# A score convolution split by row parity, with q and k taken through device memory, in an attention layer of 4 images of 32 x 32

## The reference, cut to what matters

```python
qkv = conv1x1(batchnorm(x), qkv_w, qkv_b)            # B=4, 96 channels, 32x32
q, k, v = qkv split in 3, each 6 heads of 16 channels
qk = concat([q * 16**-0.5, k], axis=1)               # 24 images (batch x head) of 32 channels
attn = conv2d(qk, dm_w, 7x7, pad 3) + dm_b + rel_bias  # 49 scores for each pixel
attn = softmax(attn, over the 49)
out = sum over the 49 window places of attn * v shifted there
x1 = x + conv1x1(out, proj_w, proj_b)
return x1 + conv1x1(gelu(conv1x1(x1, c1_w)), c2_w)
```

## Time and profile before

| | us |
|---|---|
| median of 3 runs (1281.7 to 1283.02) | 1283.01 |
| the profiled execution, its own time | 1284.04 |
| its span from first to last instruction | 1281.9 |
| the attention layer in it, from 795.9 | 486.0 |
| DVE, POOL, PE busy in the whole span | 987.5, 920.4, 1083.4 |

### The profile page before, as it was taken

One profiled execution on the slowest core, in us unless ns is written; L12 is line 12 of the kernel. 1 busy time (PEld: TensorE's weight loads), 2 busy tenths in 40 slices (PEclk: granted clock), 3 DMA queues, 4 the chain that ended last, 5 costly groups with the idle time before them and its releaser, 6 DMA issues. The chain is left out here.

```text
span 1281.9 us, 9541 instructions
## 1 busy us (share of the span) xinstructions
PE 1083.4 (85%) x3294; PEld 369.8 (29%) x3294; DVE 987.5 (77%) x695; ACT 521.1 (41%) x548; POOL 920.4 (72%) x360
## 2 busy tenths in 40 slices
PE   7789999788989889889878695899999699990567
PEld 2233333232223233223322232233333133330122
DVE  1599999789998999989899997100969694967683
ACT  5755665786646546555646341111120111010212
POOL 0189899898979798979898955100778794979770
PEclk9889999899999999999899998699999789995678
DMA  2234354434354435543435541746495549526002
GB/s 75 84 134 150 129 166 117 150 112 152 126 151 114 160 106 148 164 140 124 159 117 138 164 138 32 155 88 111 97 161 121 112 73 191 88 55 118 20 1 70
DMA packets 107640, 150.95 MB, mean 118 GB/s; under 512 B 75451, under 2 KB 76193, under 8 KB 106825
## 3 DMA queue, kind: packets, MB, share of 16 engines
q1 hardware_dynamic: 105992, 145.01, 43.4%
q10 hardware_dynamic: 1600, 5.34, 1.4%
HBM read 123.27 MB, written 10.70 MB: 105 GB/s over the span
## 5 line engine op out<-in xcount | busy, mean ns | idle before, releaser
L691 POOL TENSOR_TENSOR hc<-h,c_rep 128x1024 f32<-128x1024 f32 x192 | 450.9, 2360 | 146.6 <-DVE h L735 136.7
L735 DVE TENSOR_TENSOR_SCAN h<-a,bu 128x1024 f32<-128x1024 f32 x192 | 439.0, 2286 | 34.2 <-POOL hc L691 15.3
L389 PE MATMUL y_ps<-hc,ident 128*128 128x512 f32 x768 | 383.1, 623 | 10.8 <-POOL hc L691 9.3
L557 ACT ACTIVATE a<-dt,a_neg 128x1024 f32<-128x1024 f32 x192 | 219.2, 1146 | 251.7 <-DVE h L735 237.6
L725 DVE TENSOR_TENSOR bu<-bu,u 128x1024 f32<-128x1024 f32 x192 | 232.1, 1209 | 17.5 <-PE bu L368 17.5
L1146 POOL TENSOR_TENSOR prod_p<-vw,at 128x3584 f32<-128x3584 f32 x18 | 130.8, 7266 | 156.5 <-DMA vw<-v_d 131.1
L389 PEld LDWEIGHTS y_ps<-hc,ident 128*128 128x128 f32 x768 | 142.7, 195 | 222.2 <-issue 178.1
L1029 PE MATMUL sc_ps<-x,w_up 128*64 128x512 f32 x672 | 179.7, 609 | 2.6 <-DMA x<-qk 2.6
L1029 PE MATMUL sc_ps<-x,w_low 96*64 96x512 f32 x672 | 178.7, 606 | 0.0
L368 PE MATMUL bu<-st,pick 96*64 96x512 bf16 (+1 forms) x512 | 118.6, 391 | 51.1 <-DVE h L735 47.4
L1167 DVE TENSOR_TENSOR acc_ps<-acc_ps,prod_v 128x512 f32<-128x512 f32 x156 | 109.1, 699 | 5.4
(11 more groups left out here) (121 smaller groups left out, 940.4 us busy)
## 6 DMA issues: line engine op xcount, KB each, us to landing
c_rep<-c_d SPq DMA_DIRECT2D x128, 512.0 KB, 3.7
c_rep<-c_d SPq DMA_DIRECT2D x128, 256.0 KB, 3.9
vw<-v_d SPq DMA_DIRECT2D x24, 532.0 KB, 9.5
x<-qk SPq DMA_DIRECT2D x72, 171.0 KB, 3.7
scores_d<-sc ACTq DMA_DIRECT2D x24, 196.0 KB
at<-scores_d SPq DMA_DIRECT2D x24, 196.0 KB, 5.3
x<-qk SPq DMA_DIRECT2D x24, 152.0 KB, 3.8
v_d<-v SPq DMA_DIRECT2D x24, 76.0 KB, 5.0
```

The lines of the kernel that those rows point to most:

```text
L389: mm = pe.matmul(y_ps[:, cols(th)], ident[:, :], hc[:, k % HC_RING, cols(th)], start=(n == 0 and d == 0), stop=(n == N_ST - 1))
L557: nc.scalar.activation(a[:, k % A_RING, :], dt[:, tile % 2, :], ACT.Exp, scale=a_neg[:, kind_of(tile), n:n + 1]).then_inc(exp_done, 1)
L691: nc.gpsimd.tensor_tensor(hc[:, k % HC_RING, :], h[:, k % H_RING, :], c_rep[:, k % C_RING, :], ALU.mult).then_inc(hc_done, 1)
L735: nc.vector.tensor_tensor_scan(scan_order(h[:, k % H_RING, :], d), scan_order(a[:, k % A_RING, :], d), scan_order(bu[:, k % 2, :], d), 0.0 ...
```

## The change

**Scores by parity.** Padded rows are kept by parity in `qk` (plane 0 odd rows, plane 1 even rows). DVE adds two planes of differences of them (2 instructions for each `differences`). With the kernel's even rows as `w_even`, its odd rows as `w_odd` and their sum `w_both`, the output rows of one parity are a product shared by both, plus one of their own: three products of 14 matmuls for a pair (42 in place of 56). ACT evicts the shared one into a third plane of `sc`, and PE adds it to each of the others with a matmul by the identity (`eye`, 128 x 128), two for a pair. The scores, and all that follows down to `o_t`, are then in the order even rows, odd rows, so each `at` and `o_d` transfer of an image becomes two of 16 partitions, and `vw` reads its rows in that order.

**q and k through memory.** The planes are stored to `qk_d` and read back: one transfer fills all 128 partitions of a plane of `x4` for one image, three for an image (128, 128 and 96 partitions of 2,432 bytes). The ring has 4 images. ACT issues these loads, but for four at the start that SP issues.

**Order.** Projections of batches 1 to 3 follow pairs 0 to 2. `exps(j)` stands behind pairs 1, 3, 6, 8 and 10, the last ahead of `mlp(2)`. `maximum(j+1)` stands ahead of DVE's last row of tile j. `differences` of batch 3 stand behind `maximum(0)`. The MLP outputs on DVE are spread over tile 4 and the end of tile 5.

**VectorE sums in two banks.** The accumulator is two PSUM banks, so three additions of 1,024 elements and one of 512 take the place of seven of 512; in the first row of a tile the product of two places is written straight into them. At a tile's end one more addition joins the banks.

```diff
-X4_RING = 6
+X4_RING = 4
+EXP_AFTER = (1, 3, 6, 8, 10)
+LOAD_O = (1, 3, 4, 5)
...
+        def load_odd(eng, image):
...
+            eng.wait_ge(odd_stored[hd // 4], 16 * (b + 1))
+            src = qk_d[image, 0, 0]
+            eng.dma_start(x4[:, slot, 0, :, :].rearrange("p y x -> p (y x)"),
+                          bass.AP(src.tensor, src.offset, [[HP, 4], [3 * HH * HP, 2 * HD], [1, H // 2 * HP]]))\
+                .then_inc(odd_in[p % 2], 16)
+
+        def load_dif(eng, image):
...
+            eng.wait_ge(dif_stored[hd // 4], 16 * (b + 1))
+            for plane, taps in ((1, 4), (2, 3)):
+                src = qk_d[image, 0, plane]
+                eng.dma_start(x4[0:32 * taps, slot, plane, :, :].rearrange("p y x -> p (y x)"),
+                              bass.AP(src.tensor, src.offset, [[HP, taps], [3 * HH * HP, 2 * HD], [1, H // 2 * HP]]))\
+                    .then_inc(dif_in[p % 2], 16)
...
                 for i in range(4):
-                    sp.dma_start(at[32 * i:32 * i + 32, j % 2, :, :],
-                                 scores_d[4 * j + i].rearrange("k (y x) -> y k x", x=W)).then_inc(at_in[j % 2], 16)
+                    src = scores_d[4 * j + i]
+                    for e in range(2):
+                        sp.dma_start(at[32 * i + 16 * e:32 * i + 16 * e + 16, j % 2, :, :],
+                                     src[:, e].rearrange("k (r x) -> r k x", x=W)).then_inc(at_in[j % 2], 16)
...
-                    win = bass.AP(src.tensor, src.offset, [[V_ROW, H], [1, WIN * V_ROW]])
+                    win = bass.AP(src.tensor, src.offset, [[V_ROW, 2], [2 * V_ROW, H // 2], [1, WIN * V_ROW]])
...
-                for th in range(2):
...
+                both, even, odd = 3 * p, 3 * p + 1, 3 * p + 2
+                for n, w, rows, plane in ((both, w_both, 128, 0), (even, w_even, 128, 1), (odd, w_odd, 96, 2)):
...
                     for dx in range(WIN):
...
+                        for i in range(2):
+                            mm = pe.matmul(sc_ps[64 * i:64 * i + 64, n % 2, :], w[0:rows, dx, :],
+                                           x4[0:rows, (2 * p + i) % X4_RING, plane, :, dx:dx + W],
+                                           start=(dx == 0), stop=(n == both and dx == WIN - 1))
+                    if n != both:
+                        pe.wait_ge(sc_out, both + 1)
+                        mm = pe.matmul(sc_ps[:, n % 2, :], eye[:, :], sc[:, p % 2, 2, :], start=False, stop=True)
                     mm.then_inc(scored, 1)
...
+                if m == 0:
+                    load_odd(act, 1)
+                    load_odd(act, 3)
+                    load_dif(act, 1)
+                    load_dif(act, 3)
             for p in range(PAIRS):
                 store_scores(p)
-                if p % 3 == 0 and p // 3 + 1 < B:
+                if p + 2 < PAIRS:
+                    load_x4(p + 2)
+                if p + 1 < B:
                     for i in range(6):
-                        qkv(p // 3 + 1, i)
-            exps(TILES - 1)
+                        qkv(p + 1, i)
+                if p in EXP_AFTER:
+                    exps(EXP_AFTER.index(p))
...
+            def row(j, dy):
...
+                for k in range(2 * n - 2, WIN - 1, 2):
+                    dve.wait_ge(pv, base + n)
+                    nc.vector.tensor_tensor(acc_v, acc_v, prod_v[:, k:k + 2], ALU.add).then_inc(pv, 1)
+                    n += 1
+                dve.wait_ge(pv, base + n)
+                nc.vector.tensor_tensor(acc_v[:, 0], acc_v[:, 0], prod_v[:, WIN - 1], ALU.add).then_inc(pv, 1)
```

More of the change, by code:

```diff
@@ L783, in attention @@
 def attention(nc, t, x1, scratch):
-    scores_d, v_d, o_d = scratch
+    scores_d, v_d, o_d, qk_d = scratch
     with ExitStack() as ctx:
@@ L823, in attention @@
         prod_p = sb("prod_p", [128, WIN, HD, W])
+        zeros = prod_p[0:IMAGES].rearrange("p k c x -> p (k c x)")[:, 0:R * V_ROW]
         acc_p = sb("acc_p", [128, HD, W])
@@ L917, in _ @@
-            sp.wait_ge(zeroed, 2)
-            for side in (0, R + H):
-                sp.dma_start(v_d[:, side:side + R].rearrange("i r c x -> i (r c x)"), zeros[:, :])\
-                    .then_inc(sides, 16)
-            def put_x4(p):
-                b = p // 3
-                if p % 3 != 1:
-                    left(sp, ("qkv", b, 1 if p % 3 == 0 else 3))
-                if p >= X4_RING // 2:
-                    sp.wait_ge(scored, 2 * (p - X4_RING // 2) + 2)
-                for i in range(2):
-                    hd = 2 * (p % 3) + i
-                    for j in range(4):
-                        rows = X4_ROWS if j < 3 else H
-                        sp.dma_start(x4[32 * j:32 * j + 32, (2 * p + i) % X4_RING, 0:rows, :],
-                                     qk[32 * (hd % 4):32 * (hd % 4) + 32, hd // 4, b % 2, j:j + rows, :])\
-                            .then_inc(x4_in[p % (X4_RING // 2)], 16)
+            third = [(proj_w[:, :], t["proj_w"]), (proj_b[:, :], t["proj_b"]), (c1_w[:, :], t["c1_w"]),
+                     (c1_b[:, :], t["c1_b"]), (c2_w[:, :, :], t["c2_w"]), (c2_b[:, :], t["c2_b"])]
@@ L943, in load_tile @@
             def load_tile(j):
-                for i in range(2):
-                    sp.wait_ge(sc_stored[i], 32 * (j + 1))
                 if j >= 2:
@@ L1009, in bank, with bias @@
                 return g_ps[:, job % G_BANKS, :]
+            def bias(m):
+                n = JOB["bias", m]
+                free(n)
+                w = (slice(0, 128), slice(128, 192), slice(192, 288))[m]
+                pe.matmul(bank(n)[0:w.stop - w.start, 0:1], qkv_w[:, w], bn_shift[:, :], start=True,
+                          stop=True).then_inc(job_done, 1)
             def qkv(b, i):
@@ L1056, in _ @@
             pe.wait_ge(bn_step, BN_DONE)
-            for m, w in enumerate((slice(0, 128), slice(128, 192), slice(192, 288))):
-                n = JOB["bias", m]
-                free(n)
-                pe.matmul(bank(n)[0:w.stop - w.start, 0:1], qkv_w[:, w], bn_shift[:, :], start=True,
-                          stop=True).then_inc(job_done, 1)
-            for i in range(6):
-                qkv(0, i)
+            for m in range(3):
+                bias(m)
+                for i in range(2):
+                    qkv(0, 2 * m + i)
             pe.wait_ge(loaded[1], 16 * L1_LOADS[1])
+            pe.wait_ge(w_ready, 1)
             for p in range(PAIRS):
                 score(p)
-                if p % 3 == 0 and p // 3 + 1 < B:
+                if p + 1 < B:
                     for i in range(6):
-                        qkv(p // 3 + 1, i)
+                        qkv(p + 1, i)
+            pe.wait_ge(loaded[2], 16 * L1_LOADS[2])
             for b in range(B):
@@ L1163, in sum_v @@
-        def sum_v(dve, base, first):
-            for n in range(1 if first else 0, WIN):
-                dve.wait_ge(pv, base + n - (1 if first else 0))
-                nc.vector.tensor_tensor(acc_v, prod_v[:, 0] if first and n == 1 else acc_v, prod_v[:, n],
-                                        ALU.add).then_inc(pv, 1)
+            shifted = bass.AP(win.tensor, win.offset + lo, [list(win.ap[0]), [1, hi - lo], [HP, HD], [1, W]])
+            return engine.tensor_tensor(prod, shifted, e[:, lo:hi].unsqueeze(2).broadcast_to([128, hi - lo, HD, W]),
+                                        ALU.mult)
@@ L1247, in tile @@
                 for dy in range(DVE_ROWS[j]):
-                    base = row_start(j, dy)
+                    if dy == DVE_ROWS[j] - 1 and j + 1 < TILES:
+                        maximum(j + 1)
                     for m, i in DVE_MLP.get((j, dy), ()):
```

328 lines of the change are left out of this document (199 added, 129 removed).

## The result

The changed kernel takes 1536.6 us (median of 4 runs, 1532.4 to 1540.1) against 1282.7 of the kernel before: 1.198 times as long, with a 95% interval of 1.195 to 1.201. The prediction was 1536.

A forecast was written before the change was run, and what follows sets the result against it. Two DMA engines carrying narrow vw and x4 loads become the bound: 814 + 589 of transfers + 25 idle = 1428, then 30 + 49 + 27 = 1534 us of span, forecast 1536 us; likeliest case 1480 to 1600, full range 1255 to 1600.

The forecast's parts named there:

- The split of transfers: DMA loads: an equal split of both sides' outermost counts puts vw on two engines, x4 on four and three; narrow 0.64.
- The rate: Narrow vw and x4 loads: each DMA engine moves 25 GB/s; 13.6 as lower bound would give near 1750, 1 in 25.
- The sum: First two DMA engines: 589 us of transfers plus some 25 idle from 814, so the last vw lands near 1428.
- The two large terms: Loads on the first two DMA engines: vw 262 us over six tiles, x4 224 us over 24 images.
- the small ones: Other transfers on those engines: score stores 28 us, at 30, v stores 20, planes, o_d and o 25.
- The places of the tiles: POOL's starts of tiles 0 to 5: near 990, 1120, 1245, 1325, 1390 and 1460 us, released by vw or what follows.
- The first score: Start of scoring on PE, behind q and k's way through memory: 8 us later than 819.52, bounds 3 and 15.
- What I put beside other work: ACT's six x4 issues for a pair: 0.35 us each, 2 to 6.3 us a pair possible, lying beside PE.
- Wide: All transfers on sixteen engines, vw landing in 10 to 15 us: 1266 us, range 1255 to 1277, chance 0.27.
- the sum of tile 0: Wide, first tile from POOL's start at 905: 64.5 us of PE, scores' trip, maximum, DVE's last row and division.
- Half: vw wide, only x4 narrow: 384 us on the busiest engines, estimate 1345 us, range 1300 to 1380, chance 0.06.
- The two-bank sums: DVE's adds for a row: 4.9 us become 4.3, beside POOL's work, nothing gained at once.

The follow-up runs named there:

- e3: Changed kernel with vw read 32 rows outermost (score rows on every second partition) and x4 with 32 channels outermost: 1279.3 us, 0.996 to 1.000 of the kernel before.
- e5: Kernel before with only vw's source pattern changed to the change's, 2 rows outermost and not mergeable: 1366.5 us, 1.063 to 1.071 of before.
- e6: Kernel before with only vw's source pattern changed, three counts that can't be merged, 16 outermost: 1280.4 us, 0.997 to 1.002 of before.
- e12: e3 with each image's vw load in parity order as two transfers of 16 partitions: 1293.0 us, 1.006 to 1.012 of the kernel before.
- e1: Changed kernel with only vw made wide (32 rows outermost, score rows on every second partition), x4 left narrow: 1401.7 us, 1.090 to 1.097 of before.
- e2: Changed kernel with only x4 made wide (32 channels outermost), vw left narrow: 1416.3 us, 1.101 to 1.109 of the kernel before.
- e8: e3 with ACT's evictions of a batch's projections moved ahead of the pair's six x4 loads: 1262.4 us, 0.981 to 0.988 of the kernel before.
- e4: Kernel before with only vw's source written as two contiguous halves of 16 rows: 1283.9 us, 1.000 to 1.004 of before.

## Why the prediction was right

*The split of transfers*, the step that everything hung on, is shown: shares of 0.13 and 0.26 in the changed kernel, e3, which takes it out and gets 257 us back, and e5 against e6 in the kernel before with nothing else changed.

*The rate.* I took 25 GB/s for an engine and read the 13.6 of the earlier trace rows as a limit of the side written, which two engines don't reach. Measured were 27 for `vw` and 26 for `x4`, so they don't; e12 fits such a limit. At these rates `vw` takes 10.1 us an image where I had 10.9 (242 us for 262), and `x4` 218 for 224.

*The sum.* I had 589 us of work and 25 idle between 814 and 1428. The last of it (the `o` load behind `vw`) landed at 1425.2, after 611 us. In these 611 us there are two stretches without any transfer, 889 to 900 and about 999 to 1015, some 27 us (25 said). That leaves at most 584 us of work. The two large terms were 26 us too high together, so the small ones, with what stood idle unseen, were up to 21 us too low; no run separates these. Behind it the path is the one that I named, by the `o` load, DVE's rows and the division: 29.4 us to tile 5 on POOL (30 said), 48.7 to the last division's end (49), 27.1 of tail (27).

That 1536 was met within 1 us is luck. My own steps give 1534 + 2.1 - 1.0 = 1535. The profiled execution had a span of 1530.5, 3.5 us under my 1534, and the median of the runs lay 4.3 us above that execution's own time, where I had put it 1.0 below. Reckoned from the first engines' work in the same way, e1 came out 57 us too low and e2 91; there these engines carry less than the layer lasts.

*The places of the tiles* were the weaker part. I had 990, 1120, 1245, 1325, 1390, 1460; they came at 977, 1093, 1205, 1300, 1373, 1455: the first five 13 to 40 us early, the last nearly right. The total depends on when the two engines have carried everything, and less on the order in which they do. The first score came at 835.7, 16.2 us later than before, where I had 8 and at most 15.

*What I put beside other work.* I had six issues on ACT for a pair, 0.35 us each, beside PE's work. That failed twice. Behind narrow transfers an issue stalls (33.5 us for four). And without such a stall (e3) the six take 4.6 us, 0.76 each, and stand ahead of evictions that PE's two banks wait for: a batch's projections took 14.6 us of PE's time and not the 7 that I had in the wide rival. In the changed kernel I take that to have cost next to nothing, as the DMA's first engines were the bound; no run has it alone. e8 shows what it costs when they aren't, 17 us.

*The rivals.* Wide: 1266 said, 1279 measured in e3. The first score is right (828 said, 828.75), tiles 1 to 4 are within 1.2 us each, and what lies between is 22 us wrong, of which the 10 us that I had set aside for falls of the clock covered a part. The steps that failed are the six issues, and the sum of tile 0, which left out that the differences of batch 3 stand ahead of it. Had the transfers been wide, the change would have been a draw. Half: 1345 said, 1402 measured in e1, for the reason of `at` above.

One more gain stands in the sum of the wide case (48 us for tile 5) and not in its reason, which names two other tiles as the whole of it. Before, the last tile took 61.9 us from POOL's first product (1194.56) to the end of the division. Not POOL ended it, which was done at 1241.3, but DVE, whose first product began only behind MLP outputs:

```profile
1206.83 0.75 DVE L1225 SCALAR_TENSOR_TENSOR x<-g_ps,c_b,x 96x512 f32<-96x512 f32 x1 [9.06 <-PE g_ps L1051]
...
1209.91 3.87 DVE L1146 TENSOR_TENSOR prod_v<-vw,e_ps 128x3584 f32<-128x3584 f32 x1
```

With the MLP outputs spread as the change has them the last tile takes 48.7 us, in the changed kernel and in e3, 13 us less.

*The two-bank sums* were said to be 4.3 us a row; their rows' means of 1.23 and 0.70 us give 4.4. No run took them out alone.

## What to carry to other kernels

Look at the outermost count of both sides of every transfer, after counts that continue one another are joined: with 2 there, two engines carried it here, and what lay on all sixteen waited behind it on those two, small loads and other queues included. A rearrangement that costs nothing in instructions (every second partition as target, or channels outermost and the weights permuted to fit) gave 257 us back here. And ask of every issue and every wait in an engine's stream what evictions stand behind it: moving six issues a pair, two exponentials and five maxima, without removing one instruction, was worth 17, 13 and 16 us.

## What the runs showed of the hardware that I had not expected

- Issuing is not free of what was issued: behind narrow transfers four issues on ACT took 33.5 us and six on SP 49.1, against 0.3 to 1.2 us each in the earlier trace rows, though no semaphore wait shows there. It is not narrow transfers alone: in e3 four stores of v took SP 11.5 us at 980 us.
- A wide transfer is as late as its share on the busiest engine: `o`, 384 KB, issued right behind narrow `vw` loads, landed after 43.9 us in place of 3.6.
- A DMA share of 1 is not a speed: sixteen engines at full share moved 123 GB/s to 16 partitions and 213 to 32; `o` reached 385 with 96. The narrow loads reached 27 GB/s an engine at the same rows, twice what a wide `vw` load gets from each.
- Two counts written apart but contiguous acted as one (e4: 1283.9 us, where the same counts out of sequence in e5 took 1366.5).
